# Attention inside a fused Flamingo block: another order of scores and values on TensorE, and one set of transposed maxima where there were two

## What is computed

```python
q = (target @ Wq.T + bq).reshape(B, L, H, D).transpose(0, 2, 1, 3)   # target = layernorm(x)
k = (context @ Wk.T + bk).reshape(B, K, H, D).transpose(0, 2, 1, 3)
v = (context @ Wv.T + bv).reshape(B, K, H, D).transpose(0, 2, 1, 3)
q = _apply_rope(q, cos_q, sin_q)
k = _apply_rope(k, cos_k, sin_k)
attn = jnp.einsum('bhld,bhkd->bhlk', q, k) * scale
attn = jnp.where(context_mask[:, None, None, :], attn, -jnp.inf)
attn = jax.nn.softmax(attn, axis=-1)
x = jnp.einsum('bhlk,bhkd->bhld', attn, v)
```

## Time and profile before

| | before |
|---|---|
| median of 3 runs | 808.38 us |
| the profiled execution | 809.36 us |
| its span, first to last instruction | 807.4 us |
| mean granted clock of TensorE | 0.935 |
| busy in the span: PE / DVE / ACT / POOL | 706.4 / 473.1 / 373.3 / 286.0 us |
| attention, from the first pair to the last values | 108.4 to about 318 us |

### The profile page before, as it was taken

The page is one execution under the profiler, slowest core; times in us unless marked ns, Lnnn a source line. Parts: engine busy times, 40 slices in busy tenths (PEclk is TensorE's granted clock), DMA queues, the critical chain, the costliest instruction groups (busy, mean ns, idle before and its releaser), DMA issues. The chain is left out here.

```text
span 807.4 us, 11568 instructions
## 1 busy us (share of the span) xinstructions
PE 706.4 (87%) x3970; PEld 454.7 (56%) x3970; DVE 473.1 (59%) x852; ACT 373.3 (46%) x660; POOL 286.0 (35%) x477
## 2 busy tenths in 40 slices
PE   3699969999999997869899999998489999966886
PEld 1377734444444443754678787776266766752454
DVE  3576667787778760653844343434346546457985
ACT  0166635888888887435432232342222130202565
POOL 2355623434434432283001010010122346247797
PEclk9699977999999999898999999999598998996999
DMA  6001000000000001910020000000200000000001
GB/s 192 13 30 30 13 8 1 1 2 1 2 1 1 2 1 55 392 37 1 0 105 1 1 1 0 0 1 0 65 1 0 1 1 1 1 0 0 27 32 46
DMA packets 14106, 21.49 MB, mean 27 GB/s; under 512 B 2160, under 2 KB 11504, under 8 KB 13296
## 3 DMA queue, kind: packets, MB, share of 16 engines
q1 hardware_dynamic: 13200, 20.34, 7.5%
q10 hardware_dynamic: 864, 0.59, 0.2%
HBM read 18.83 MB, written 2.10 MB: 26 GB/s over the span
## 5 line engine op out<-in xcount | busy, mean ns | idle before, releaser
L564 DVE TENSOR_REDUCE mx<-ps_f 128x2 f32<-128x1024 f32 x128 | 150.2, 1219 | 45.1 <-PE ps_f L496 45.1
L639 ACT ACTIVATE prob<-ps_s 128x512 f32<-128x512 f32 x256 | 141.1, 603 | 33.4 <-PE ps_s L515 31.3
L515 PE MATMUL ps_s<-q_stacks,k_stacks 64*128 64x512 f32 x256 | 104.3, 459 | 0.3 <-ACT prob L639 0.3
L528 PE MATMUL ps_o<-prob,vst 128*32 128x256 f32 (+1 forms) x896 | 79.1, 426 | 0.7 <-ACT prob L639 0.4
L515 PEld LDWEIGHTS ps_s<-q_stacks,k_stacks 64*128 64x128 f32 x256 | 43.8, 188 | 60.0 <-ACT prob L639 28.2
L496 PE MATMUL ps_f<-k_stacks,q_stacks 64*128 64x512 f32 x256 | 66.1, 461 | 6.8 <-DVE mx L564 5.3
L1020 ACT ACTIVATE qs<-ps_g 128x512 f32<-128x512 f32 x40 | 23.9, 598 | 89.3 <-PE ps_u L904 89.3
L1087 DVE SCALAR_TENSOR_TENSOR h<-ps_u,most,qs 128x512 f32<-128x512 f32 x32 | 24.0, 751 | 62.6 <-ACT qs L1020 62.6
L589 POOL TENSOR_TENSOR q_stacks<-minus,q_stacks 128x512 fp32r<-128x512 f32 x32 | 40.6, 1272 | 43.5 <-ACT minus L630 43.5
L172 POOL TENSOR_TENSOR norm_tmp_att<-st 128x4 f32<-128x4 f32 x4 | 1.0, 238 | 142.5 <-DVE st L1126 142.5
L1529 ACT ACTIVATE qs<-ps_SC,nmax 128x512 f32<-128x512 f32 x16 | 11.0, 687 | 77.0 <-DVE nmax L1417 76.9
(11 more groups left out here) (278 smaller groups left out, 1573.5 us busy)
## 6 DMA issues: line engine op xcount, KB each, us to landing
up<-in_up SPq DMA_DIRECT2D x10, 256.0 KB, 6.7
x<-in_x SPq DMA_DIRECT2D x4, 512.0 KB, 8.1
ctxT<-in_ctxT SPq DMA_DIRECT2D x16, 128.0 KB, 2.0
ks<-in_ctxTC SPq DMA_DIRECT2D x1, 2048.0 KB, 11.9
ks<-in_ctx SPq DMA_DIRECT2D x1, 2048.0 KB, 18.1
out<-x SPq DMA_DIRECT2D x16, 128.0 KB, 1.7
down<-in_down SPq DMA_DIRECT2D x1, 1280.0 KB, 5.6
ks<-in_wqv SPq DMA_DIRECT2D x1, 1024.0 KB, 20.1
```

What stands on the lines that cost most here:

```text
L515: pe.matmul(ps_s[n % 3][:, :], ks[rows(h), 2 * s + pair, kt * P:(kt + 1) * P], qs[rows(h), 2 * s + pair, :], start=True, stop=True).then_i ...
L528: last = pe.matmul(ps_o[HPAD * j:HPAD * (j + 1), cols], vst[:, s % 2, kt, HPAD * j:HPAD * (j + 1)], prob[:, kt % 2, j, cols], start=(kt == 0),
L564: dve.tensor_reduce(mx[:, f % 2, qt, 2 * pair:2 * pair + 2], ps_f[n % 2][:, :, :], AX_X, ALU.max).then_inc(used, 1)
L639: act.activation(prob[:, kt % 2, j, :], ps_s[n % 3][:, :], ACT.Exp, scale=SCALE)\
```

## The change

There are four parts.

1. On TensorE a block is now: scores 0 and 1, a pair, (in kt = 2 the transposes,) score 2, a pair, score 3, then the values whole, 512 columns.
2. The maxima of both pairs of heads go into one set of four transposes. `mt` has two places in place of four: head h of either pair shares a place, the first pair's high and low part in the rows 48 and 49, the second's in 50 and 51. So the transposed rows hold both pairs' maxima. The mask row moves to 52. In k the ones stand in 48 and 49 for the first pair of heads and in 50 and 51 for the second, so that each pair picks its own.
3. ScalarE copies one slot instead of two, and GpSimd lowers both stacks in one addition of 128x1024 whose operand `minus` is read twice.
4. A step has 17 items in the slots instead of 18, and the slots are numbered anew. ScalarE's copy stands ahead of its third exponential in kt = 2.

```diff
-MAX_ROW, MASK_ROW = 3 * HD, 3 * HD + 2
+MAX_ROW, MASK_ROW = 3 * HD, 3 * HD + 4
...
 def score_slot(s, kt, j):
-    added = (0, 0, 1 + j // 2, 2)[kt] if s + 1 < STEPS else 0
-    return 2 + (QT * G + 2) * s + G * kt + j + added
+    added = (0, 0, j // 2, 1)[kt] if s + 1 < STEPS else 0
+    return 1 + (QT * G + 1) * s + G * kt + j + added
...
-def max_slot(f, pair):
-    return score_slot(f - 1, 2, 2 * pair) - 1 if f else pair
+def max_slot(f):
+    return score_slot(f - 1, 2, 1) + 1 if f else 0
...
-        mt = sb("mt", [P, 2, QT, G, ROWS], F32)
-        minus = sb("minus", [P, 2, S], F32)
+        mt = sb("mt", [P, 2, QT, 2, ROWS], F32)
+        minus = sb("minus", [P, 1, S], F32)
...
                 for j in range(G):
-                    last = pe.matmul(ps_o[HPAD * j:HPAD * (j + 1), cols], vst[:, s % 2, kt, HPAD * j:HPAD * (j + 1)],
-                                     prob[:, kt % 2, j, cols], start=(kt == 0),
-                                     stop=(kt == QT - 1 and half == 1))
-                if half or kt == 0:
-                    last.then_inc(pv_done, 1)
+                    last = pe.matmul(ps_o[HPAD * j:HPAD * (j + 1), :], vst[:, s % 2, kt, HPAD * j:HPAD * (j + 1)],
+                                     prob[:, kt % 2, j, :], start=(kt == 0), stop=(kt == QT - 1))
+                last.then_inc(pv_done, 1)
...
-                pe.wait_ge(lowered, 2 * (s + 1))
+                pe.wait_ge(lowered, s + 1)
                 for kt in range(QT):
-                    before = divmod(s * QT + kt - 1, QT)
-                    for j in range(G):
-                        if kt == 2 and j % 2 == 0 and s + 1 < STEPS:
-                            maxima(s + 1, j // 2)
-                        scores(s, kt, j)
-                        ahead = UNITS * s + LEAD + 2 * kt + j
-                        if j < 2 and ahead < UNITS * STEPS:
-                            first_scores(ahead)
-                        if j >= 2 and s + kt:
-                            values(*before, j - 2)
+                    ahead = UNITS * s + LEAD + 2 * kt
+                    scores(s, kt, 0)
+                    scores(s, kt, 1)
+                    if ahead < UNITS * STEPS:
+                        first_scores(ahead)
+                    if kt == 2 and s + 1 < STEPS:
+                        maxima(s + 1)
+                    scores(s, kt, 2)
+                    if ahead + 1 < UNITS * STEPS:
+                        first_scores(ahead + 1)
+                    scores(s, kt, 3)
+                    if s + kt:
+                        values(*divmod(s * QT + kt - 1, QT))
...
-            def lower(f, pair):
-                pool.wait_ge(slot_read, max_slot(f, pair) + 1)
-                own = qs[:, 2 * f + pair, :]
-                pool.tensor_tensor(own, minus[:, pair, :], own.bitcast(F32), ALU.add).then_inc(lowered, 1)
+            def lower(f):
+                pool.wait_ge(slot_read, max_slot(f) + 1)
+                own = qs[:, 2 * f:2 * f + 2, :]
+                pool.tensor_tensor(own, minus[:, :, :].broadcast_to([P, 2, S]), own.bitcast(F32), ALU.add)\
+                    .then_inc(lowered, 1)
```

More of the change, by code:

```diff
@@ L377, in _ @@
             pool.memset(stack[:, :, 0, :, MASK_ROW:MASK_ROW + 1], 1.0)
-            pool.memset(stack[:, :, 1, :, MAX_ROW:MAX_ROW + 2], 1.0).then_inc(preset, 1)
+            in_pairs = stack[:, :, 1, :, :].rearrange("p u (a b) r -> p u a b r", b=4)
+            for pair in range(2):
+                at = MAX_ROW + 2 * pair
+                last = pool.memset(in_pairs[:, :, :, 2 * pair:2 * pair + 2, at:at + 2], 1.0)
+            last.then_inc(preset, 1)
             ln_pool(pool, 0, (0, QT))
@@ L498, in first_scores, with maxima @@
                 last.then_inc(filled, 1)
-            def maxima(f, pair):
-                n = max_slot(f, pair)
+            def maxima(f):
+                n = max_slot(f)
                 pe.wait_ge(mt_ready, f + 1)
@@ L516, in scores, with values @@
                           qs[rows(h), 2 * s + pair, :], start=True, stop=True).then_inc(slot_done, 1)
[L518 to L526, removed]
-                for j in range(G):
-                    last = pe.matmul(ps_o[HPAD * j:HPAD * (j + 1), cols], vst[:, s % 2, kt, HPAD * j:HPAD * (j + 1)],
-                                     prob[:, kt % 2, j, cols], start=(kt == 0),
-                                     stop=(kt == QT - 1 and half == 1))
-                if half or kt == 0:
-                    last.then_inc(pv_done, 1)
+            def values(s, kt):
+                pe.wait_ge(slot_read, score_slot(s, kt, G - 1) + 1)
+                if kt == 0:
+                    pe.wait_ge(v_ready, s + 1)
+                    wait(pe, o_copied, s)
+                for j in range(G):
+                    last = pe.matmul(ps_o[HPAD * j:HPAD * (j + 1), :], vst[:, s % 2, kt, HPAD * j:HPAD * (j + 1)],
+                                     prob[:, kt % 2, j, :], start=(kt == 0), stop=(kt == QT - 1))
+                last.then_inc(pv_done, 1)
             for n in range(UNITS + 2):
                 first_scores(n)
-            for pair in range(2):
-                maxima(0, pair)
+            maxima(0)
             for n in range(UNITS + 2, LEAD):
@@ L540, in _ @@
             for s in range(STEPS):
[L541 removed]
+                pe.wait_ge(lowered, s + 1)
                 for kt in range(QT):
[L543 to L554 removed]
+                    ahead = UNITS * s + LEAD + 2 * kt
[11 more added lines that the diff above has]
+                        values(*divmod(s * QT + kt - 1, QT))
+            values(STEPS - 1, QT - 1)
         @block.vector
@@ L612, in _ @@
             split(0)
-            for pair in range(2):
-                lower(0, pair)
+            lower(0)
             for s in range(STEPS):
@@ L619, in _ @@
                     split(s + 1)
-                    for pair in range(2):
-                        lower(s + 1, pair)
+                    lower(s + 1)
                 bias(s)
@@ L625, in _, with copy_maxima @@
         def _(act):
-            def copy_maxima(f, pair):
-                n = max_slot(f, pair)
+            def copy_maxima(f):
+                n = max_slot(f)
                 act.wait_ge(slot_done, n + 1)
-                wait(act, lowered, 2 * (f - 1) + pair + 1)
-                act.copy(minus[:, pair, :], ps_s[n % 3][:, :]).then_inc(slot_read, 1)
+                wait(act, lowered, f)
+                act.copy(minus[:, 0, :], ps_s[n % 3][:, :]).then_inc(slot_read, 1)
             def exps(s, kt):
@@ L635, in exps @@
                     n = score_slot(s, kt, j)
-                    if kt == 2 and j % 2 == 0 and s + 1 < STEPS:
-                        copy_maxima(s + 1, j // 2)
+                    if kt == 2 and j == 2 and s + 1 < STEPS:
+                        copy_maxima(s + 1)
                     act.wait_ge(slot_done, n + 1)
@@ L645, in sums_out @@
                 act.copy(o32[:, s, 0:S], ps_o[:, :]).then_inc(o_copied, 1)
-            for pair in range(2):
-                copy_maxima(0, pair)
+            copy_maxima(0)
             for s in range(STEPS):
```

13 lines of the change are left out of this document (7 added, 6 removed).

## The result

The changed kernel takes 795.38 us (median of 4 runs, 794.62 to 796.35), against 808.73 us for the kernel before in the same measurement (806.57 to 809.79). The ratio is 0.984, with a 95% interval of 0.9815 to 0.9863: 1.6% faster, 13 us. The prediction was 795.5.

What follows compares the result with a forecast made beforehand. TensorE's order of work set the pace; afterwards a score-exponential-score-values loop would. Full steps -11.2, start and s = 0 -2.0, last steps +0.3: -12.9 from 809.36 gives 796.5, median 795.5 us; forecast 789 to 801, range 787 to 803.5.

Steps and rivals of the forecast that it cites:

- The loop: Plain block: first score, its exponential, fourth score (1.24 us), values (0.43), next block's first score (0.99); 2.66 in all.
- The plain blocks: Blocks kt = 0, 1 and 3 of a step: 7.95 us before, 8.00 after, so nothing won there.
- The block kt = 2: Block with the transposes: one set and one copy on ScalarE removed, 3.14 us against 4.05; 3.4 at the late end.
- The two bounds for the set's start: In kt = 2, when the remaining transposes start after the first score: between 0.46 and 0.90 us, taken as 0.5 to 0.65.
- The steps: The 13 full steps, s = 1 to 13: 11.14 us each against 12.00, -11.2 us in all.
- The start and s = 0: Attention's start and first step: four fewer transposes and shorter blocks, -2.0 us in all, with ends 0 and -2.7.
- The last steps: s = 14 and 15: blocks without pairs lengthen from 2.25 to 2.66 us, 21.48 to 21.8 in all, +0.3.
- D: Loop holds but a link is longer, 0.1 us more per block, 6 us in all; 801 to 811 us, chance 0.14.
- A: Fourth score doesn't wait; TensorE's own work is the pace, plain block 2.15 us, total 769; chance 0.05.
- B: TensorE's clock falls because the new wait idles it 0.2 to 0.3 us per block; 812 to 830 us, chance 0.05.
- C: GpSimd's wide addition is slow, deciding the pace from 4.5 us against 2.5 taken; 806 to 820 us, chance 0.03.

Runs made afterwards that it cites:

- short_exp0: Changed kernel with the first exponential of each block (head 0, from step 1 on) taking 256 of its 512 columns; 783.34 us, ratio 0.968.
- short_exp2: Changed kernel with the third exponential of each block (head 2, from step 1 on) taking 256 of its 512 columns; 793.17 us, ratio 0.981.
- one_set: Changed kernel with the order of scores and halved values of before, but the one set of transposes ahead of score 2 in kt = 2; 801.84 us.
- order_only: Kernel before with TensorE's new order alone; the two sets of transposes, two copies and two additions stay; 804.22 us, ratio 0.994.
- halves: Changed kernel with the values in two halves again, one ahead of score 3 and one behind it; 800.59 us, ratio 0.989.
- double_set: Changed kernel with each of the four transposes of maxima issued twice in a row from step 1's on; 799.07 us, ratio 0.988.

## Why the prediction was right

**The loop.** Forecast 1.24, 0.43, 0.99, sum 2.66; measured 1.24, 0.43, 0.99 in the block at 292.77 and 2.67 in the blocks with pairs. It was read off the blocks without pairs of the kernel before, where the same wait already showed, and short_exp0 and short_exp2 confirm that it is a cause and not a coincidence. TensorE's own work is only 0.2 shorter than the loop.

**The plain blocks win nothing.** Forecast 7.95 to 8.00, measured 8.04.

**The block kt = 2.** Forecast 3.14, measured 3.16 in the step shown. The two bounds for the set's start were 0.46 and 0.90, I took 0.5 to 0.65, it was 0.66. The third score came at +1.25 by the end of the set and by the exponential at once, the fourth at +1.73 (forecast +1.72).

**What the text said of its cause was incomplete.** I put the 0.91 down to the set removed and the copy. one_set shows that the set taken away alone is worth 0.33 over kt = 1 and 2, and the order alone 0.12; together they give 0.74. In the new order the set is worth its 0.59 and the copy with the rest 0.04 (order_only). In the old order half of the 0.59 goes to a wait that it had covered: the second pair then waits for VectorE, and the set behind it starts 0.33 later than in the changed kernel. The slot of the late score, which I had taken for the reason, costs 0.04 (halves). The size was right since the block was worked out link by link in the new order, but the one set tried alone in the old order would have foretold only 0.33.

**The sum.** The steps gave -10.3 and not -11.2: 0.07 too little for each step, of which kt = 1 (2.70 for 2.68), kt = 2 (3.18 on average for 3.14), and kt = 0 and 3 (2.67 for 2.66) all have a part. The start and s = 0 gave -1.9 (forecast -2.0), made of 0.9 in the start, where the four transposes take 1.04 in place of 1.89, and 1.0 in s = 0. The granted clock rose somewhat later than I had taken it to: between 132 and 134 us it was 0.52, against 0.91 before. The last steps gave +0.4 (forecast +0.3). Together -11.8 for -12.9. That the median agreed to 0.1 us is luck: the rest of the kernel was 1.7 shorter in this profile than in the one before, and it differs between 594 and 598 us over the eleven profiled executions of this study, with nothing changed in it but the small fills at its start. The chances of D, 0.14, went into the shares of faster and same as 0.13; no other number hangs on it.

**The rivals.** A (TensorE's own work is the pace, 769 us) is out: order_only has the fewer changes between kinds and its plain blocks take the loop's 2.66. A was also priced too low. Its 1.16 + 0.99 = 2.15 leaves out the fourth score, which takes 0.33 at the end of a row (double_set) and 0.39 in short_exp0; TensorE's own work is 2.46 there and the time 783.34, not 769. VectorE's two reductions, 2.36 in a row, are close as well. The rule of the Trainium skill that was weighed there ("TensorEngine Tiling (Array Packing)", Key Properties, a change of mode drains the engine) is not contradicted, but the page states no price, and the 0.42 that I read as one is none by itself: in the changed kernel a fourth score costs 0.43 with no change of mode ahead of it, only a wait. No run here tells a drain from other costs. B (a falling clock) didn't come: 1.00 from s = 1 on, with an idle stretch in each block. C (a slow wide addition) didn't come: 2.37 on average, a little less than two additions of 1.27. D (a link longer by 0.1) didn't come: the links were within 0.01 to 0.04 (the longest miss is the fourth score of kt = 1, at +1.27 for 1.24).

## What to carry to other kernels

Before a group of work is moved behind an instruction that waits, ask which wait it used to cover. Take the loop through the slots link by link from the rows, with the time from a producer's start to its reader's start, since those links hardly change when the order does. And when two edits meet in one block, work out the block with both in it: here they gave 1.6 and 6.0 us of the attention apart, and 11.8 together. Ask for each engine whether it still keeps up in the shorter block: what swallowed half of the removed set in one_set was VectorE, which had kept up before. Last, a list of waits counts a queue's idle time also where the engine behind it is busy; only a run that shortens the wait tells what it costs.

## What the runs showed that I had not expected

Two scores on different halves of the array's rows, put side by side, shortened the group ahead of the values by only 0.04 us (1.12 for 1.16): before, score 0 had started together with a matmul of the first pair.

A reduction of 512 columns takes little more than half of one of 1024 (0.60 from start to start, four in 2.48, against 1.14, two in 2.36), so splitting the pairs cost VectorE little time; what it cost was the third of three banks, since a block's fourth first score needs the bank of its first.
